# Cross-attention with feed-forward: attention in duos of two batch pairs on TensorE's tiles, rotation summed on GpSimd

## The reference

```python
x = x + attention(layernorm(x), ctx, ctx, pos, mask)   # x, ctx: 32 batches x 64 rows x 512
x = x + ffn(layernorm(x))
# attention: q = h @ Wq (32 heads of 128), k = ctx @ Wk, v = ctx @ Wv (8 heads of 128 each)
q = q * cos + rotate_half(q) * sin                     # k likewise; cos, sin by position
scores = where(mask == 0, -1e9, q @ k.T / sqrt(128))   # four query heads share a key head
out = softmax(scores) @ v; return out @ Wo
# ffn: routing = softmax(h @ gate_w.T)                 # 8 experts
out = ((h * (routing @ in_scale)) @ sign(weight).T) * (routing @ out_scale) + bias
```

## Time and profile before

| | |
|---|---|
| Median of 3 runs | 1336.24 us (1334.14 to 1336.83) |
| Profiled execution | 1334.63 us, span 1332.4 us, mean granted clock 0.985 |
| TensorE matmul busy | 1244.2 us, 93% of the span |
| VectorE busy | 1058.8 us, 79% |
| ScalarE busy | 817.8 us, 61% |
| GpSimd busy | 594.2 us, 45% |

### The profile page before, as it was taken

How to read it: one execution, slowest core, us unless ns; L and a number is a source line. 1 busy time by engine, 2 the same in 40 slices (tenths; PEclk the granted TensorE clock), 3 DMA queues, 4 the chain that set the end, 5 groups by cost and what they waited for, 6 DMA issues and landing times.

```text
span 1332.4 us, 22295 instructions
## 1 busy us (share of the span) xinstructions
PE 1244.2 (93%) x6228; PEld 1027.7 (77%) x6228; DVE 1058.8 (79%) x1815; ACT 817.8 (61%) x2280; POOL 594.2 (45%) x435
## 2 busy tenths in 40 slices
PE   6799999999999999999899999999999999999977
PEld 5677777887777788777788877887777788877755
DVE  6688888777888877887787888888778887887754
ACT  4666666665666666565665566766666676566632
POOL 5344444333455434544333564443445444454324
PEclk9899999999999999999899999999999999999987
DMA  7233332222322222332322332222222212222100
GB/s 211 62 100 107 98 91 76 72 69 72 107 80 79 63 79 63 115 99 76 87 62 61 95 92 66 78 79 87 79 88 79 64 55 70 72 87 77 49 1 32
DMA packets 136919, 105.88 MB, mean 79 GB/s; under 512 B 12776, under 2 KB 111080, under 8 KB 136864
## 3 DMA queue, kind: packets, MB, share of 16 engines
q1 hardware_dynamic: 131488, 94.78, 24.6%
q10 hardware_dynamic: 4608, 8.39, 1.9%
q0 software_dynamic: 768, 2.10, 0.5%
HBM read 101.05 MB, written 4.19 MB: 79 GB/s over the span
## 4 chain that ended last, share of the span: by engine, by line
PE 61%; DVE 25%; issue 7%; ACT 4%; POOL 1%; DMA 0%; DVEq 0%; ACTq 0%; POOLq 0%; SPq 0%
PE chunk L1019 14%; PE chunk L1021 14%; PE chunk L1020 14%; PE sc_ps L1063 8%; DVE swp L772 6%; DVE qT L784 4%; DVE rot L771 4%; DVE kT L784 4%; ACT swp L467 3%; PE tr_ps L1008 3%; DVE pT_lo L711 2%; PE aux L1008 2%; PE o_ps L1021 1%; PE o_ps L1019 1%; PE o_ps L1020 1%
## 5 line engine op out<-in xcount | busy, mean ns | idle before, releaser
L384 POOL TENSOR_TENSOR w_lo<-raw,w_hi 128x512 fp32r<-128x512 f32 x192 | 266.3, 1394 | 550.2 <-ACT w_hi L467 550.1
L502 ACT ACTIVATE probs<-scores,neg_max 128x64 f32<-128x64 f32 x512 | 171.9, 337 | 108.2 <-DVE neg_max L732 107.3
L384 POOL TENSOR_TENSOR wo_lo<-raw,wo_hi 128x512 fp32r<-128x512 f32 x132 | 218.8, 1668 | 40.9 <-ACT wo_hi L467 40.9
L1019 PE MATMUL chunk<-wo_hi,oT_hi 128*128 128x512 f32 x512 | 210.8, 412 | 0.0
L467 ACT ACTIVATE swp<-chunk 64x512 f32<-64x512 f32 x320 | 189.9, 594 | 29.8 <-DVE qT L784 18.5
L1021 PE MATMUL chunk<-wo_hi,oT_lo 128*128 128x512 f32 x512 | 201.4, 393 | 0.0
L1019 PE MATMUL chunk<-xT_hi,w_hi 128*128 128x512 f32 (+1 forms) x512 | 200.5, 392 | 0.0
L1020 PE MATMUL chunk<-wo_lo,oT_hi 128*128 128x512 f32 x512 | 200.3, 391 | 0.0
L1021 PE MATMUL chunk<-xT_hi,w_lo 128*128 128x512 f32 (+1 forms) x512 | 200.0, 391 | 0.0
L1020 PE MATMUL chunk<-xT_lo,w_hi 128*128 128x512 f32 (+1 forms) x512 | 199.4, 389 | 0.0
L467 ACT ACTIVATE pT_hi<-tr_ps 64x256 fp32r<-64x256 f32 x256 | 96.9, 378 | 115.5 <-PE o_ps L1021 104.3
(11 more groups left out here) (268 smaller groups left out, 2303.6 us busy)
## 6 DMA issues: line engine op xcount, KB each, us to landing
raw<-in_L_xattn_Wo SPq DMA_DIRECT2D x132, 256.0 KB, 2.6
raw<-in_L_xattn_Wq SPq DMA_DIRECT2D x128, 256.0 KB, 2.7
raw<-in_L_xattn_Wk SPq DMA_DIRECT2D x32, 256.0 KB, 2.9
raw<-in_L_xattn_Wv SPq DMA_DIRECT2D x32, 256.0 KB, 2.7
acc<-in_x ACTq DMA_DIRECT2D x16, 256.0 KB, 2.7
c_tile<-in_ctx SPq DMA_DIRECT2D x12, 256.0 KB, 3.5
x_tile<-in_x SPq DMA_DIRECT2D x12, 256.0 KB, 3.8
result<-y ACTq DMA_DIRECT2D x12, 256.0 KB, 2.1
```

Source lines behind the costliest of these rows:

```text
L384: nc.gpsimd.tensor_tensor(lo, raw[:, n % RING, :], hi.bitcast(F32), ALU.subtract).then_inc(wsplit_lo, 1)
L502: last = nc.scalar.activation(e[:, k, :], scores[:, p, bass.ts(k, S)], ACT.Exp, bias=neg_max[:, p % 2, k:k + 1], accum_out=ssum[:, p % 2, ...
L1019: nc.tensor.matmul(bank, a_hi, b_hi, start=i == 0, stop=False)
```

## The change

- **Duos.** The attention goes in two steps instead of four, each with two pairs. A duo's scores fill all 512 columns of `sc_ps`; mask, maximum, product, `pT_hi` and `pT_lo` are one operation each with twice the columns (the last two also with 128 partitions instead of twice 64), and the exponentials come in groups of eight.
- **Scores** are column-tiled: each matmul has 64 weight columns (the queries of one head) and writes 64 partitions, so there are twice as many.
- **Values** are row-tiled: for each pair, part and batch a matmul over that batch's 64 rows with 256 columns; batch 0 writes bank 0 of `o_both`, batch 1 bank 1. pT has no zeros any more, and the two memsets go. Both banks belong to one duo: `values(s, 1)` waits for `out_lo` of pairs 0 and 1 of the same slot.
- **Rotation.** `rotate` writes the cos product straight into kT or qT; GpSimd's `rope_sum` adds swp to it in place and counts `roped`. `swap` waits for `roped` as before, so swp is free only after GpSimd's sum. The buffer `rot` goes.
- The orders in the four `slot` functions are written anew.

```diff
-        neg_max = sb("neg_max", [P, 2, 4])
...
-        in_raw, out_raw, gate_raw = vT, probs[:, :, :, :, :].rearrange("p k a b t -> p (k a b t)"), c_tile
+        in_raw, out_raw, gate_raw, sign_scratch = vT, probs[:, 0, :], c_tile, probs[:, 1, :]
...
-        o_ps = [stack.enter_context(nc.psum_tensor(f"o_ps{i}", [P, 512], F32)) for i in range(2)]
+        o_both = stack.enter_context(nc.psum_tensor("o_ps", [P, 2, 512], F32))
+        o_ps = [o_both[:, i, :] for i in range(2)]
...
+        def heads_of_o(p):
+            return o_both[:, :, bass.ts(p % 2, HG * S)].rearrange("p b (h s) -> p b h s", h=HG)
+        def rope_out(j):
+            if j == 0:
+                return kT[:, :], lambda ap: ap
+            h = j - 1
+            dst = qT[:, h // 2, :].rearrange("p (b a s) -> p b a s", a=2, s=S)[:, :, h % 2, :]
+            return dst, lambda ap: ap.rearrange("p (b s) -> p b s", s=S)
...
-            for zeros in (gate_raw[:, :], in_raw[:, :], out_raw, route[:, :], pT_hi[:, :, :].bitcast(F32), pT_lo[:, :, :].bitcast(F32)):
+            for zeros in (gate_raw[:, :], in_raw[:, :], out_raw, route[:, :]):
...
+            def rope_sum(s, j):
+                pool.wait_ge(sin_done, s.U * KQ + j + 1)
+                dst, by_batch = rope_out(j)
+                nc.gpsimd.tensor_tensor(dst, dst, by_batch(swp[:, j % 2, :]), ALU.add).then_inc(roped, 1)
...
-                    for n in range(3, 7):
-                        split_lo(s, n)
+                    split_lo(s, 3)
+                    split_lo(s, 4)
                 if s.first_proj:
                     wait_alone(pool, rows_tr, PAIRS)
                     nc.gpsimd.memset(scores[:, :, :], MASKED).then_inc(fill_ok, 1)
+                if s.proj:
+                    rope_sum(s, 0)
+                    split_lo(s, 5)
+                    split_lo(s, 6)
+                    rope_sum(s, 1)
+                    split_lo(s, 7)
+                    rope_sum(s, 2)
                 if s.ffn:
                     xs_lo_split(f[0], in_slot)
                 if s.proj:
-                    for n in range(7, CH):
-                        split_lo(s, n)
+                    split_lo(s, 8)
+                    rope_sum(s, 3)
+                    split_lo(s, 9)
+                    rope_sum(s, 4)
...
-            def exp_pair(s, p):
-                n = (s.U - 1) * PAIRS + p
+            def exp_duo(s, d):
+                n = (s.U - 1) * DUOS + d
                 act.wait_ge(maxed, n + 1)
-                if not (s.first_attn and p < 2):
+                if not s.first_attn:
                     act.wait_ge(probs_tr, n - 1)
-                e = probs[:, p % 2, :, :, :].rearrange("p a b t -> p (a b) t")
-                for k in range(4):
-                    last = nc.scalar.activation(e[:, k, :], scores[:, p, bass.ts(k, S)], ACT.Exp,
-                                                bias=neg_max[:, p % 2, k:k + 1], accum_out=ssum[:, p % 2, k:k + 1])
+                for k in range(8):
+                    last = nc.scalar.activation(probs[:, d, bass.ts(k, S)], scores[:, 2 * d + k // 4, bass.ts(k % 4, S)], ACT.Exp,
+                                                bias=neg_max[:, d, k:k + 1], accum_out=ssum[:, d, k:k + 1])
                 last.then_inc(exped, 1)
...
-            def pT_hi_split(s, p):
-                n = (s.U - 1) * PAIRS + p
+            def pT_hi_split(s, d):
+                n = (s.U - 1) * DUOS + d
                 act.wait_ge(probs_tr, n + 1)
-                if not (s.first_attn and p == 0):
+                if not (s.first_attn and d == 0):
                     act.wait_ge(pv_done, n)
-                copy(pT_hi[0:S, 0, :], tr_ps[0:S, 0:2 * P])
-                copy(pT_hi[S:P, 1, :], tr_ps[S:P, 0:2 * P]).then_inc(pT_h, 1)
+                copy(flat2(pT_hi), tr_ps[:, :]).then_inc(pT_h, 1)
...
-                n = (s.U - 1) * PAIRS + p
-                if p == 0 and isinstance(s.g, int) and s.g == 1:
+            def soft_a(s, d):
+                n = (s.U - 1) * DUOS + d
+                if d == 0 and isinstance(s.g, int) and s.g == 1:
                     dve.wait_ge(mask_in, 32 * (s.q + 1))
                     dve.wait_ge(fill_ok, s.q + 1)
                 wait_alone(dve, scores_done, n + 1)
+                sc = scores[:, 2 * d:2 * d + 2, :]
                 nc.vector.copy_predicated(
-                    scores[:, p, :].rearrange("p (a n) -> p a n", a=2),
-                    msk[:, p, :].unsqueeze(1).to_broadcast([P, 2, P]),
-                    sc_ps[:, 0:2 * P].rearrange("p (a n) -> p a n", a=2)).then_inc(masked, 1)
+                    sc.rearrange("p i (a n) -> p i a n", a=2),
+                    msk[:, 2 * d:2 * d + 2, :].unsqueeze(2).to_broadcast([P, 2, 2, P]),
+                    sc_ps[:, :].rearrange("p (i a n) -> p i a n", i=2, a=2)).then_inc(masked, 1)
                 dve.wait_ge(masked, n + 1)
-                nc.vector.tensor_reduce(neg_max[:, p % 2, :], scores[:, p, :].rearrange("p (a t) -> p a t", t=S),
+                nc.vector.tensor_reduce(neg_max[:, d, :], sc.rearrange("p i (a t) -> p (i a) t", t=S),
...
-                dve.wait_ge(pT_h, (s.U - 1) * PAIRS + p + 1)
-                lo_of(pT_lo[0:S, 0, :], tr_ps[0:S, 0:2 * P], pT_hi[0:S, 0, :])
-                lo_of(pT_lo[S:P, 1, :], tr_ps[S:P, 0:2 * P], pT_hi[S:P, 1, :]).then_inc(pT_l, 1)
+            def pT_lo_split(s, d):
+                dve.wait_ge(pT_h, (s.U - 1) * DUOS + d + 1)
+                lo_of(flat2(pT_lo), tr_ps[:, :], flat2(pT_hi)).then_inc(pT_l, 1)
             def out_lo(s, p):
-                dve.wait_ge(o_hi, (s.U - 1) * PAIRS + p + 1)
-                lo_of(oT_lo[:, p, :, :].rearrange("p h (b s) -> p b h s", b=2),
-                      o_ps[p % 2][:, :].rearrange("p (b h s) -> p b h s", b=2, h=HG),
+                dve.wait_ge(o_hi, (s.U - 1) * PAIRS + p // 2 * 2 + 2)
+                lo_of(oT_lo[:, p, :, :].rearrange("p h (b s) -> p b h s", b=2), heads_of_o(p),
                       oT_hi[:, p, :, :].rearrange("p h (b s) -> p b h s", b=2)).then_inc(o_lo, 1)
             def rotate(s, j):
...
                 k = j % 2
                 here = span(s.side * BT, BT)
-                if s.first_proj and j == 0:
-                    dve.wait_ge(fw_sgn, EC)
-                else:
-                    dve.wait_ge(roped, n)
-                dve.wait_ge(swapped, n + 1)
-                nc.vector.tensor_tensor(rot[:, :], chunk[PROJ_BANK[j]][:, :], cosT[:, here], ALU.mult).then_inc(cos_done, 1)
+                dst, by_batch = rope_out(j)
+                if s.attn and j == 0:
+                    dve.wait_ge(scores_done, s.U * DUOS)
+                dve.wait_ge(swapped, s.U * KQ + j + 1)
+                nc.vector.tensor_tensor(dst, by_batch(chunk[PROJ_BANK[j]][:, :]), by_batch(cosT[:, here]), ALU.mult).then_inc(cos_done, 1)
                 nc.vector.tensor_tensor(swp[:, k, :], swp[:, k, :], sinT[:, here], ALU.mult).then_inc(sin_done, 1)
-                if s.attn and j == 0:
-                    dve.wait_ge(scores_done, s.U * PAIRS)
-                dve.wait_ge(cos_done, n + 1)
-                dve.wait_ge(sin_done, n + 1)
-                if j == 0:
-                    dst, a, b = kT[:, :], rot[:, :], swp[:, k, :]
-                else:
-                    h = j - 1
-                    dst = qT[:, h // 2, :].rearrange("p (b a s) -> p b a s", a=2, s=S)[:, :, h % 2, :]
-                    a = rot[:, :].rearrange("p (b s) -> p b s", s=S)
-                    b = swp[:, k, :].rearrange("p (b s) -> p b s", s=S)
-                nc.vector.tensor_tensor(dst, a, b, ALU.add).then_inc(roped, 1)
...
                 for p in range(PAIRS):
                     last = transpose(tr_ps[:, bass.ts(p, D)], vT[:, bass.ts(p, P)])
                 last.then_inc(v_tr, 1)
-            def scores_of(s, p):
-                n = (s.U - 1) * PAIRS + p
+            def scores_of(s, d):
+                n = (s.U - 1) * DUOS + d
                 pe.wait_ge(roped, s.U * KQ)
-                if not (s.first_attn and p == 0):
+                if not (s.first_attn and d == 0):
                     pe.wait_ge(masked, n)
-                for hp in range(HG // 2):
-                    for b in range(2):
-                        at = 2 * p + b
-                        last = nc.tensor.matmul(sc_ps[:, bass.ts(2 * hp + b, S)], qT[:, hp, bass.ts(at, P)],
-                                                kT[:, bass.ts(at, S)], start=True, stop=True)
+                for p in (2 * d, 2 * d + 1):
+                    for hp in range(HG // 2):
+                        for b in range(2):
+                            at, place = 2 * p + b, 4 * (p % 2) + 2 * hp + b
+                            for a in range(2):
+                                queries = slice(at * P + a * S, at * P + (a + 1) * S)
+                                last = nc.tensor.matmul(sc_ps[a * S:(a + 1) * S, bass.ts(place, S)],
```

(90 more changed lines are left out.)

62 lines of the change are left out of this document (22 added, 40 removed).

## The result

The median of eleven runs is **1342.44 us** (1337.97 to 1343.86) against 1334.99 (1333.81 to 1336.83) for the kernel before: 1.0049 of it, 95% interval 1.0039 to 1.0060. The forecast was 1315, faster; it is slower by 0.5%. The profiled execution has a span of 1340.8 us at a mean clock of 0.98.

What follows compares the result with a forecast made beforehand. TensorE was taken as the bound, with waits made by VectorE's rotations. Plain slot 32.6 + 2S + 2V = 35.9 us; 7 x -1.3 + 12 x 1.0 - 12 x 2.0 = -21 us off the median gives 1315, range 1264 to 1386.

Steps and rivals of the forecast that it cites:

- Scores: Forecast step on column-tiled score matmuls: two column tiles work at once, a duo's 1.7 us becomes 0.9 with a start.
- Values: Forecast step on row-tiled value matmuls: both row tiles work at once, a duo's 1.56 us becomes 0.75.
- S: TensorE's time to get through the scores of a duo, twice in a slot; forecast 0.9 us.
- V: TensorE's time for the value products of a duo, twice in a slot; forecast 0.75 us.
- rival of drains: Eight changes of array shape in a slot cost TensorE 0.16 us each, 1.3 in all: 1355 us; chance 0.10.
- one after another: Rival: tiles of scores and values do not overlap, plain slot 38.9 us, 1384 us in all; chance 0.20.
- one kind only: Rival: only column tiles or only row tiles overlap, 1340 to 1358, about 1345 us; chance 0.13.
- Dearer scores: Rival: a load of 64 weight columns costs as much as 128, 0.103 us; above 1460 us; chance 0.04.
- (a): Plain slot, duo 1's probabilities: ready 6.6 us after its scores, so TensorE waits 0.7 us before their transposes.
- (b): Plain slot, duo's single bank pair: values(1) waits 1.55 us until both oT_lo of duo 0 are read.
- (c), (d): Plain slot after values(1): swap(2), then GpSimd's split 7 to split 9, ending at 18.0 + 2V; out_proj(0) waits about 1.6 us.
- The added waits are hidden: Rival: GpSimd splits earlier, out_proj(0) does not wait, slot 34.3 us, 1265 us in all; chance 0.13.

Runs made afterwards that it cites:

- untiled runs: Changed kernel with column tiling undone, 1362.0 us, or row tiling undone, 1369.1; fastest kernel (all orders moved, xs's split ahead of sum 2) with both undone, 1278.3.
- alternating run: Changed kernel with a duo's scores half untiled (128 weight columns), half column-tiled (64), in alternation: 1396.5 us.
- grouped run: Changed kernel with the same tiled matmuls reordered, all of one tile first, then all of the other, in scores and values: 1393.2 us.

## Why the prediction was wrong

**The step that failed** is in *Scores* and *Values*: "I take both halved, S = 0.9 and V = 0.75". Halved they are, between entry and exit; what I left to a rival was the cost of getting in and out, for which the forecast has 0.05 us in S and nothing in V. Measured, with what is ahead of and behind the records: S = 0.09 (slower entry) + 1.08 + 0.02 = 1.19, V = 0.09 + 0.91 + 0.11 = 1.11. (The 1.08 and 0.91 are medians over the 62 duos with all their records in the trace, from the first record to the next block; the rest is what the start before and the one behind are wider than in the untiled runs.) Put into the formula, 32.6 + 2 x 1.19 + 2 x 1.11 is **37.2** us, and the plain slot takes 37.14; S + V = 2.30 is the break-even that I had worked out. Two terms were 0.65 us too small together, and 1.3 us a slot was all of the gain.

**The rival of drains** had the right cause, a price for each change of shape, and the right sum for a slot, 1.3 us. That the sum fits is in part luck: its 0.16 was how far a record runs past the next start, and the 1.3 us is spread otherwise, 0.09 on each way in, the rest in the way out and in records that stand a little wider than half (0.93 for 32 score starts instead of 0.85). The alternating run shows a change apart from all else, 0.15. By the rule that I weighed there (the Trainium skill, TensorEngine Tiling (Array Packing), Key Properties), changing the tiling mode drains TensorE, while different tiles work in parallel. The traces agree with both halves: 0.15 us for a change, and starts on two tiles 3 to 6 ns apart; what TensorE does in the 0.15 us no record shows. I had given this rival 0.10. Its time, 1355, is 13 above what came.

**Overlap** was right: column-tiled scores and row-tiled values each run at once, and *one after another* and *one kind only* fall with the grouped run. *Dearer scores* falls too: a load of 64 columns costs 58 ns, not 103.

**The waits** of a plain slot came in the places forecast, two of them smaller: (a) probs_T(1), 0.7 forecast, 0.35 idle by the timeline; (b) values(1), 1.55 and 1.14; (c), (d) out_proj(0), 1.6 and 1.66; project(5)'s wait gone. *The added waits are hidden* falls there. I counted split 9 from swap(2) on, and in the changed kernel that is how it goes: from one out_proj(0) to values(1) the formula gives 23.5 us with the measured S and V and the timeline 23.4, to split 7 29.9 and 29.4. With values(1) earlier and splits 3 and 4 later, though, out_proj(0) waited longer (34.5 us against 27.7), so there the order ahead of split 7 came to bear.

**Slots.** Forecast and measured, against before: the feed-forward slots -24 and -3.7 us, plain -9 and -5.3, intake +12 and +13.3.

Two of the seven plain slots make up all of the -5.3: the first (35.8 to 32.4 us, at a granted clock of 0.86 before and 0.95 now) and one that follows a feed-forward slot (37.2 to 35.2). The other five take what they took, so the forecast gain of 1.3 in each is not there.

Nearly all of the miss is in the feed-forward slots: 38.9 forecast, 40.2 with the 1.3 us, and most of them take 40.3. That this fits so well is partly luck, for the path in them is not the one that I had summed, GpSimd's with the split of xs in it. The end of one of them:

```profile
509.65 0.47 PE L1161 MATMUL aux<-sgnT,xs_hi 128*128 128x512 f32 x1 [0.28 <-POOL xs_lo L424]
...
511.58 0.39 PE L1011 MATMUL chunk<-cT_hi,w_hi 128*128 x1
...
512.41 1.30 POOL L396 TENSOR_TENSOR wo_lo<-raw,wo_hi 128x512 fp32r<-128x512 f32 x1
...
514.33 0.39 PE L1011 MATMUL chunk<-wo_hi,oT_hi 128*128 128x512 f32 x1
```

Split 9 is done at 513.71, and out_proj(0) starts 0.6 us later without a wait. While GpSimd works off its chain, TensorE has the feed-forward's matmuls too, the product between project(4) and project(5) alone 1.9 us, and the sum had none of those; so there TensorE's own work sets the time. It also shows why the first feed-forward slot of each four takes 41.4 to 41.8: its out_proj(0) waits 1.6 to 2.0 us for GpSimd's chain of the intake or plain slot before it.

In intake the forecast 39.3 with the 1.3 us would be 40.6, and nine of the twelve take 39.7 to 40.1, with about the forecast waits for the probabilities (1.7 forecast, 1.6 measured) and for GpSimd. What is missing is the 1.3 of waiting for the rope tables: no such wait in nine slots, at most 0.8 in three. So +12 for these slots came out nearly right by two errors that cancel, and the rival's 1355 was not reached.

Not tried: the zeros of the block-diagonal operand in the untiled runs, which would change the copies of pT, so the 46 us of the tiles are for TensorE's side alone.

## What to carry to other kernels

Small tiles of the array pay where many of them stand together: count entry and exit as two terms of their own (here 0.09 in, and 0.02 or 0.11 out beside what is in the records), and issue neighbours on different tiles. In a loop over in-order engines, work freed on the bounding engine shows up as time only after the waits behind the others' orders are moved as well: one move alone gave -46, two cost 10 and 38, and a kernel with all three waits taken out, with a new stream of weights too, gave -96. Look at the granted clock slot by slot before you put such a cost down to waits: the clock made up about all of the +10. And a move of work between engines must be judged in the order that it will stand in; the sums on GpSimd cost 24 us in one and saved 19 in the other.
